# A product's moving operand stored with the token tile outermost, in the two feed-forward fronts

## The reference, cut to what matters

```
scores = sigmoid(h @ gate_w.T)                 # h: (4096, 256) after layernorm
topk_score, topk_ids = top_k(scores.T, 512)    # for each of 16 experts
xin = h[topk_ids]
eo  = (silu(xin @ gw.T + gb) * (xin @ up_w.T + up_b)) @ down_w.T + down_b
out = scatter_add(eo * topk_score) + shared(h) # shared: silu(h @ a.T) * (h @ b.T) @ c.T
x   = x + 0.5 * out
```

## Time and profile before

| | value |
|---|---|
| median of three runs | 2378.57 us |
| profiled execution, time | 2372.61 us |
| profiled execution, span | 2370.8 us |
| TensorE matmul busy | 2214.9 us, 93% |
| TensorE weight load busy | 1931.6 us, 81% |
| VectorE busy | 1680.5 us, 71% |
| ScalarE, GpSimd busy | 902.3 us and 884.7 us |
| mean granted TensorE clock | 0.961 of full speed |

### The profile page before, as it was taken

The page is one execution under the profiler, slowest core; times in us unless marked ns, Lnnn a source line. Parts: engine busy times, 40 slices in busy tenths (PEclk is TensorE's granted clock), DMA queues, the critical chain, the costliest instruction groups (busy, mean ns, idle before and its releaser), DMA issues. The chain is left out here.

```text
span 2370.8 us, 38149 instructions
## 1 busy us (share of the span) xinstructions
PE 2214.9 (93%) x13596; PEld 1931.6 (81%) x13596; DVE 1680.5 (71%) x3681; ACT 902.3 (38%) x1673; POOL 884.7 (37%) x920
## 2 busy tenths in 40 slices
PE   6998999999999699947999999968998999999998
PEld 5887888888889477736889999967887888888887
DVE  5785777777777588865766666645776777777775
ACT  5221333333333477722333333335222333333332
POOL 4201233333322589813524444434201333232332
PEclk9998999999999799968999999989998999999999
DMA  5003455355443411113424444443013445444442
GB/s 181 28 28 115 117 126 135 110 141 127 118 134 79 124 59 41 39 51 83 87 51 85 84 86 86 66 106 103 32 36 119 134 111 145 126 119 129 127 134 45
DMA packets 154108, 228.05 MB, mean 96 GB/s; under 512 B 33344, under 2 KB 104512, under 8 KB 153920
## 3 DMA queue, kind: packets, MB, share of 16 engines
q1 hardware_dynamic: 103664, 158.42, 21.5%
q0 software_dynamic: 39936, 55.93, 13.6%
q10 hardware_dynamic: 10320, 11.27, 1.4%
HBM read 171.16 MB, written 54.39 MB: 95 GB/s over the span
## 5 line engine op out<-in xcount | busy, mean ns | idle before, releaser
L1184 ACT ACTIVATE me_act_f<-me_in,me_bias 128x512 f32<-128x512 f32 (+1 forms) x192 | 119.2, 621 | 298.0 <-PE me_in L142 295.5
L1184 ACT ACTIVATE f2e_silu<-f2e_in,f2e_bias 128x512 f32<-128x512 f32 (+1 forms) x136 | 90.3, 664 | 340.5 <-PE f2e_in L142 293.1
L1184 ACT ACTIVATE f1e_silu<-f1e_in,f1e_bias 128x512 f32<-128x512 f32 (+1 forms) x136 | 90.3, 664 | 339.9 <-PE f1e_in L142 291.7
L140 PE MATMUL f2e_in<-f2e_xt_hi,f2e_w_hi 128*128 128x512 f32 (+1 forms) x544 | 208.5, 383 | 4.0 <-DVE f2e_xt_lo L1252 2.3
L140 PE MATMUL f1e_in<-f1e_xt_hi,f1e_w_hi 128*128 128x512 f32 (+1 forms) x544 | 208.5, 383 | 3.9 <-DVE f1e_xt_lo L1252 2.3
L142 PE MATMUL f1e_in<-f1e_xt_hi,f1e_w_lo 128*128 128x512 f32 (+1 forms) x544 | 207.8, 382 | 0.0
L142 PE MATMUL f2e_in<-f2e_xt_hi,f2e_w_lo 128*128 128x512 f32 (+1 forms) x544 | 207.7, 382 | 0.0
L141 PE MATMUL f1e_in<-f1e_xt_lo,f1e_w_hi 128*128 128x512 f32 (+1 forms) x544 | 207.4, 381 | 0.0
L141 PE MATMUL f2e_in<-f2e_xt_lo,f2e_w_hi 128*128 128x512 f32 (+1 forms) x544 | 207.1, 381 | 0.0
L140 PE MATMUL me_down<-me_w_hi,me_act_hi 128*128 128x256 f32 x640 | 184.0, 288 | 0.0
L141 PE MATMUL me_down<-me_w_lo,me_act_hi 128*128 128x256 f32 x640 | 180.2, 282 | 0.0
(11 more groups left out here) (459 smaller groups left out, 7001.0 us busy)
## 6 DMA issues: line engine op xcount, KB each, us to landing
f_raw<-in_ffn_w SPq DMA_DIRECT2D x256, 384.0 KB, 3.6
m_raw<-in_moe_w SPq DMA_DIRECT2D x64, 256.0 KB, 2.9
f1s_x_all<-in_x SPq DMA_DIRECT2D x8, 512.0 KB, 7.4
after_ffn<-f1s_out SPq DMA_DIRECT2D x8, 512.0 KB, 2.9
after_moe<-ma_x_all SPq DMA_DIRECT2D x32, 128.0 KB, 1.7
m_h<-ma_h SPq DMA_DIRECT2D x32, 128.0 KB, 1.7
f2s_x_all<-after_moe SPq DMA_DIRECT2D x8, 512.0 KB, 7.9
out<-f2s_out SPq DMA_DIRECT2D x8, 512.0 KB, 3.1
```

Source lines behind the costliest of these rows:

```text
L140: pe.matmul(out, lh, rh, start=first, stop=False, skip_group_check=True)
L1184: act.activation(dst[:, st % 2, 0:n], ps_in[st % 2][0][:, 0:n], func, bias=bias[:, b, f:f + 1]).then_inc(silu_done, 1)
```

## The change

One word of the layout of `moved` changes, in `ffn_front`, which both layers run. Before, the 64 values of x are innermost: columns of one product (fixed x) are 64 elements, 128 bytes, apart, and one expert row's token tiles lie side by side. After, x is outermost: the 64 columns of one product lie side by side, and token tiles of one row are 64 elements apart. So `slots` reads its moving operand as one run, and `move` writes each element 128 bytes from the one before it. What `move` reads, what `slots` loads, the counts, sizes, addresses of the buffers and the order of all instructions stay.

```
-        moved = [a.bitcast(F16).rearrange("p (r f x) -> p r f x", r=R, f=4)
+        moved = [a.bitcast(F16).rearrange("p (x r f) -> p r f x", r=R, f=4)
                  for a in (raw[:].rearrange("p f w -> p (f w)")[:, 0:4 * GC], x_all[:, 0:8].rearrange("p t d -> p (t d)"))]
```

## The result

The changed kernel takes 2415.69 us (median of four runs, 2411.81 to 2417.98) beside 2376.82 us for the kernel before (four runs, 2372.23 to 2379.89): a ratio of 1.0165, 95% interval 1.0151 to 1.0179. It is 38.9 us slower; forecast were 6.1 us less. The profiled execution has a span of 2416.2 us, 45.4 more than before, at a mean clock of 0.950.

What follows compares the result with a forecast made beforehand. TensorE was taken as the bound, with VectorE also full in a plain step at each front's end. Sets -9.5, stalls +8.1, low clock +2.0, clock returned -6.7 made -6.1 us: 2372.5 us from 2378.57, range 2364 to 2386 (8 in 10).

Steps and rivals of the forecast that it cites:

- I take 3.75: In `move`: an instruction writing 2048 elements at the new stride takes 3.75 us, between ends of 1.22 and 7.3.
- The rival of two accesses per element: In `move`: a half-precision strided write costs twice the strided price, 7.3 us; 2386.8 us in all; chance 0.08.
- The halved rate alone: Rival in `move`: the strided half-precision write costs only the halved rate, 2.29 us; 2364.6 us in all; chance 0.17.
- `move(1)` costs nothing: In step 29 of each front: `move(1)`, 5.06 us longer, is needed only at `down(28)` and `into(31)`, ten us on.
- The cover of 5.16 us: Behind `move(1)` in step 29: VectorE idles 5.16 us before the next `add_shared`, while TensorE has its first set.
- a slack of 1.03 us: In each front: `activation_low(25)` ends at 166.27 and `down(25)` begins at 167.30, so 1.03 us of delay is free.
- the 4.03 I booked: In each front: TensorE ends 4.03 us late from `move(0)` growing by 5.06; two fronts make +8.1 us.
- 2.89 us forecast: In `slots`: each of the eight sets takes 2.89 us, with 88 ns per product, in place of 4.7 or 3.5.
- the load already sets the 110: Rival in `slots`: weight loads set the 110 ns pace, so only `moved[0]` sets shorten; 2382.4 us; chance 0.16.
- the products stay as they are: Rival in `slots`: 110 and 147 ns come from the weights alone, so only cost is left; 2388.7 us; chance 0.06.
- 9.5 + 6.7 = 16.2 us: In the fronts: eight shorter sets save 9.5 us, and two thirds of 10.0 us lost to low clocks return, 6.7.
- 8.1 + 2.0 us: At `down(24)` in two fronts: stalls from the longer `move` cost 8.1 us, low clocks after the waits 2.0.

Runs made afterwards that it cites:

- line 701: Unread VectorE probe added to the kernel before, TensorE idle: two-input multiply writing 2048 half-precision elements 128 bytes apart; 9.26 us.
- line 706: Unread VectorE probe added to the kernel before; its time for 2048 elements is 2.29 us.
- the lighter variants: The changed kernel with `move` walking otherwise, or `moved` in runs of two, four or eight token tiles: -2.7, -12.5, -16.2, -4.8 us against the kernel before.
- the turned walk: The changed kernel with `move` walking x outermost, so writing side by side and reading strided; -2.7 us against the kernel before (0.9973 to 0.9999).
- runs of four: The changed kernel with four token tiles side by side in `moved`, a product's columns 8 bytes apart; -16.2 us against the kernel before (0.9909 to 0.9952).
- the dead writes alone: The kernel before with an unread strided half-precision write ahead of each of `move`'s instructions; 2419.03 us against 2375.38, ratio 1.0195.

## Why the prediction was wrong

**The step that failed is the size of the write**, "I take 3.75", with 7.3 us as the upper end: measured are 9.5. The nearest row was single precision, whose whole words cost 0.71 ns more per element at that stride; half-precision numbers alone in their place cost some 4.5 ns in all. I priced the element, and the price hangs on how much of a word it fills. The path from there, through VectorE's queue to `down(24)`, was right: `move(0)` grew by 16.26 us, and less the 0.36 of slack told below that is the wait of 15.9 at `down(24)`. The rival of two accesses per element had the right direction and the point from which it decides (5.3 us), with a chance of 0.08 and a price still too low. The halved rate alone is what 4 bytes apart shows (2.43 us, though 512 visits at 4.5 ns would give that as well), and not 128. By the Trainium skill ("VectorE: DVE Perf Modes", "What auto-detection actually checks") the engine takes two half-precision elements at once only if every tensor has a step of one. The 9.26 us of line 701 are far more than the loss of that would be, by the 2.29 us for 2048 of line 706.

**"`move(1)` costs nothing" failed with it.** The cover of 5.16 us would hold for 5.06 us more, and none of the lighter variants shows a wait there; `move(1)` grew by 16.4, and TensorE waited 8.7 at `down(28)`, which waits for `add_shared` as `down(24)` does. My warning, up to 5 us per front if that cover were gone, was not carried into the sum.

**What `down(24)` waits for was misnamed.** I took `activation_low(24)` and a slack of 1.03 us. The wait ends with `add_shared`, one instruction further; neither the words on the kernel nor the prediction name that wait, which stands in the code as `if f == 0 and g: pe.wait_ge(out_done, g)`. `add_shared` had ended at 162.78 before, 0.36 us ahead of `down(24)` at 163.14, as VectorE's timeline of the kernel before shows:

```profile
161.50 1.28 DVE L604 SCALAR_TENSOR_TENSOR f1s_out<-f1s_down,f1s_x_all 128x512 f32<-128x512 f32 x2
```

With 5.06 us of growth that makes 4.70, and the turned walk, with a move 5.2 us longer, waited 4.85 and 4.81; the 4.03 I booked were 0.7 too low per front.

**Right, with the size:** the sets (2.89 us forecast, 2.85 to 2.91 measured), and that the moving reads set the old pace and the loads the next; the rivals in which the load already sets the 110, or the products stay as they are, fall with the 90 ns. Right in kind: fewer low clocks behind the sets, and a low clock in the wait and behind it. My gain without the move's cost, 9.5 + 6.7 = 16.2 us, is near what runs of four show, with `move` at its old price: 16.2, by its interval 11 to 22, of which the sets give 9.1. That both say 16.2 is luck. So the sum failed by its cost: 8.1 + 2.0 us forecast. Measured, the stretch to `down(28)` grew by 22.6 us per front although three quarters of the sets' gain (3.65 of 4.86 us) stand inside it; the dead writes alone cost 43.6.

**The range failed with the bound.** I took twice a neighbour's price as an upper end for an operation that no row showed; 2386 us was no more than that guess.

## What to carry to other kernels

A layout that helps the reader can move its stride to the writer. Price a strided write of two inputs by how many 16-byte places it enters, and by whether it fills whole words there; where no row shows its price, time it alone first, as line 701 did. Then look for the layout between the two. Here runs of four (8 bytes) left the write at its old price and the read hidden behind the load. In a stage where two engines are both full, a slower one takes the bound, and gains of the other within that stage are worth nothing until the price is gone.

## What the runs showed of the hardware

- A two-input VectorE instruction that writes half-precision numbers each alone in its 16 bytes took about 4.5 ns per element (9.26 us for 2048), with single precision 1.76 (3.60 us); side by side 0.6 and 1.1 ns. A copy with one source and the same strided write took 4.72 us.
- TensorE's moving reads in half precision cost 1.7 to 1.95 ns per column 128 or 16 bytes apart, and at most 0.94 ns 8 bytes apart (160 columns in 150 ns). A load of 128 columns 128 bytes apart allowed a product every 90 ns, of columns 8 bytes apart one every 62.
- The collision of `moved[0]` and `hot[0]` (147 ns against 110) was gone in every layout tried, even at 16 bytes, where reads bind. I have no explanation that a run tests.
